# Graph attention and hyperbolic mean on one core: one folded weight matrix for the scores, normalisation moved to GpSimd

## What is computed

```python
h = relu(layernorm(x))                      # layer 0: attention inside graphs
query, key, value = h @ Wq.T + bq, h @ Wk.T + bk, h @ Wv.T + bv
a = where(mask, query @ key.T / sqrt(256), 0)
scores = (a + adj + adj) * where(mask, 1, -1e6)
x = x + (softmax(scores) * mask) @ value
h = relu(layernorm(x))                      # layer 1: weighted mean over all rows
x = x + gnn1(h, adj, W)                     # its core is adj @ (gamma * points)
```

## Time and profile before

| what | value |
|---|---|
| median of 3 runs | 795.56 us (793.64 to 797.42) |
| the profiled execution | 796.11 us |
| its span | 794.3 us |
| PE busy in the span | 740.1 us, 93% |
| DVE busy | 639.8 us, 81% |
| ACT busy | 480.7 us, 61% |
| POOL busy | 100.1 us, 13% |
| mean granted TensorE clock | 0.979 |

### The profile page before, as it was taken

How to read it: one execution, slowest core, us unless ns; L and a number is a source line. 1 busy time by engine, 2 the same in 40 slices (tenths; PEclk the granted TensorE clock), 3 DMA queues, 4 the chain that set the end, 5 groups by cost and what they waited for, 6 DMA issues and landing times.

```text
span 794.3 us, 14768 instructions
## 1 busy us (share of the span) xinstructions
PE 740.1 (93%) x4996; PEld 684.3 (86%) x4996; DVE 639.8 (81%) x1240; ACT 480.7 (61%) x879; POOL 100.1 (13%) x212
## 2 busy tenths in 40 slices
PE   4999979999999999999878899999999999999980
PEld 4888868788888888888778899999999999999980
DVE  6768577877787878889689788988888888888874
ACT  2344356787777789778654555555544555555853
POOL 0000121122111112268000000000000000000080
PEclk9999989999999999999999999999999999999995
DMA  5116268767777776679737698999899889999541
GB/s 146 54 54 239 106 246 300 273 241 253 289 289 288 281 258 253 238 255 220 171 74 154 155 204 188 202 201 199 185 218 195 189 188 190 189 192 204 120 154 63
DMA packets 53000, 157.26 MB, mean 198 GB/s; under 512 B 8656, under 2 KB 30416, under 8 KB 46800
## 3 DMA queue, kind: packets, MB, share of 16 engines
q1 hardware_dynamic: 52944, 156.60, 72.1%
HBM read 148.16 MB, written 8.42 MB: 197 GB/s over the span
## 4 chain that ended last, share of the span: by engine, by line
PE 44%; issue 28%; DVE 10%; POOLq 5%; DMA 5%; ACT 3%; DVEq 2%; POOL 1%; SPq 1%; ACTq 0%
PE bank L676 42%; DMA adjL<-in_adj 3%; DVE adjT_lo L1503 3%; DMA x_scratch<-x 1%; POOLq L600 1%; DVE bank L1495 1%; DVE turned L1495 1%; ACT adjT_hi L1018 1%; POOLq L620 1%; PE bank L668 1%; POOLq L606 1%; POOLq L550 1%; DVE X_lo L1483 1%; POOL q_low L558 1%; DMA w_raw<-in_L_gnn_Wv 1%
## 5 line engine op out<-in xcount | busy, mean ns | idle before, releaser
L676 PE MATMUL bank<-X_hi,adjT_hi 128*128 128x258 f32 x1024 | 291.6, 285 | 14.2 <-DVE adjT_lo L1503 14.2
L676 PE MATMUL bank<-X_lo,adjT_hi 128*128 128x258 f32 x1024 | 290.8, 284 | 0.0
L676 PE MATMUL bank<-X_hi,adjT_lo 128*128 128x258 f32 x1024 | 290.2, 283 | 0.0
L676 PEld LDWEIGHTS bank<-X_hi,adjT_hi 128*128 128x128 f32 x1024 | 194.4, 190 | 16.7 <-DVE adjT_lo L1503 13.6
L676 PEld LDWEIGHTS bank<-X_lo,adjT_hi 128*128 128x128 f32 x1024 | 194.8, 190 | 0.0
L676 PEld LDWEIGHTS bank<-X_hi,adjT_lo 128*128 128x128 f32 x1024 | 194.6, 190 | 0.0
L822 PE MATMUL bank<-values,probT 128*128 128x256 f32 x512 | 120.7, 380 | 1.1 <-ACT probT L1142 1.1
L1018 ACT CAST adjT_hi<-turned 128x1024 fp32r<-128x1024 f32 x64 | 67.1, 1048 | 68.0 <-PE bank L676 56.5
L822 PEld LDWEIGHTS bank<-values,probT 128*128 128x128 f32 x512 | 92.9, 189 | 14.2 <-ACT probT L1142 2.1
L1018 ACT CAST adjT_hi<-bank 128x1024 fp32r<-128x1024 f32 x64 | 64.8, 1013 | 62.3 <-PE bank L676 44.2
L1495 DVE STREAM_TRANSPOSE bank<-adjL 128x1024 f32<-128x1024 f32 x61 | 76.2, 1250 | 16.3 <-DMA adjL<-in_adj 15.9
(11 more groups left out here) (195 smaller groups left out, 1125.7 us busy)
## 6 DMA issues: line engine op xcount, KB each, us to landing
adjL<-in_adj SPq DMA_DIRECT2D x120, 512.0 KB, 8.5
adjU<-in_adj SPq DMA_DIRECT2D x32, 1024.0 KB, 7.5
adjL<-in_adj SPq DMA_DIRECT2D x16, 2048.0 KB, 7.9
x_scratch<-x SPq DMA_DIRECT2D x16, 258.0 KB, 3.4
xin<-in_x SPq DMA_DIRECT2D x8, 512.0 KB, 3.9
xt<-in_x SPq DMA_DIRECT2D x16, 256.0 KB, 7.0
adj<-in_adj SPq DMA_DIRECT2D x8, 512.0 KB, 14.0
x_all<-x_scratch SPq DMA_DIRECT2D x16, 256.0 KB, 10.7
```

What stands on the lines that cost most here:

```text
L676: last = pe.matmul(dst, a[i][a_cols], b[j][b_cols], start=(k_first and n == 0), stop=(k_last and n == 2))
```

## The change

The scores are `(h Wq' + bq)(h Wk' + bk)'`. Written out they are `h (Wq' Wk) h'`, plus a term of the column that is `bq Wk h'`, plus a term of the row `h Wq' bk + bq bk'`. The kernel after makes `Wq' Wk` once (4 matmuls from the raw weights), multiplies the group's rows by it with `bq Wk` as bias, and calls that the queries. The keys are the normalised rows themselves, which are there already: the high and low parts of the turned rows in the upper four groups, and their relu in the lower ones (`keys_lower`, on ACT). The term of the row is a 257th column of the values (a 258th is a copy of it, so that the count is even): the values' weights get two more columns, `Wq' bk`, and DVE adds the row's number in `scores_lower`, `maximum_upper` and the bias of the upper exponential.

`normalise` and `diagonal` go from DVE to POOL. Statistics and normalisation of group g+2, not g+1, are made during `project(g)`. The turning of group g+1 stands between the two halves of the queries. The three weights are not turned any more but for the values'. The check of the graph borders stands behind DVE's `project(1)`, and the sums that give `graph_col` ahead of it all. The order of the first loads is kept but for the last weight `W`, which comes behind the second group of rows. Attention is otherwise as before, and the mean is not touched.

```diff
+        wT_hi = place("wT_hi", [P, 2, KD, XW], "adjL", N * 4 + 2 * BPC * D * 4, F32R)
+        wT_lo = place("wT_lo", [P, 2, KD, XW], "small", 0, F32R)
...
+        value_banks = [a[:, :].rearrange("p (j c) -> p j c", j=2)[:, :, 0:XW] for a in (bank34, bank67)]
...
+            def normalise(g):
+
+                par = g % 2
+                pool.wait_ge(s_rstd, g + 1)
+                for j in range(BPC):
+                    last = pool.tensor_scalar(xin[:, par, j, :], xin[:, par, j, :], mv[:, par, j, 0:1],
+                                              rstd[:, par, j:j + 1], ALU.subtract, ALU.mult)
+                last.then_inc(s_norm, 1)
+
+            def diagonal(g):
+
+                pool.wait_ge(s_col, 1)
+                wait(pool, s_grow_ps, g - 1)
+                for j in range(BPC):
+                    t = g * BPC + j
+                    last = pool.tensor_scalar(diag[:, g % 2, j * P:(j + 1) * P], ident_b[:, :],
+                                              graph_col[:, t:t + 1], None, ALU.mult)
+                last.then_inc(s_diag, 1)
+
+            normalise(0)
+            normalise(1)
+            diagonal(0)
+            for g in range(NG):
+                if g < NG - 2:
+                    normalise(g + 2)
+                if g < NG - 1:
+                    diagonal(g + 1)
+            pool.wait_ge(s_kq, KD * (NG // 2 + 1))
...
+            pe.wait_ge(s_wqk, 16 * 2)
+            for k in range(KD):
                 for h in range(KD):
...
+                    last = pe.matmul(bank[2][:, k * D:(k + 1) * D], w_raw[:, 0, h, k * P:(k + 1) * P], w_raw[:, 1, h, :],
+                                     start=(h == 0), stop=(h == KD - 1))
+            last.then_inc(s_fold_ps, 1)
+            pe.wait_ge(s_wv, 16)
+            for h in range(KD):
+                for k in range(KD):
+                    last = pe.transpose(bank[3][:, k * D + h * P:k * D + (h + 1) * P],
+                                        w_raw[:, 2, h, k * P:(k + 1) * P], ident[:, :])
+            last.then_inc(s_wt_ps, 1)
+
+            def folded_biases():
+
+                pe.wait_ge(s_wide, 1)
+                for k in range(KD):
+                    for h in range(KD):
+                        pe.matmul(bank[4][:, k:k + 1], w_raw[:, 1, h, k * P:(k + 1) * P], bqk[:, 0, h:h + 1],
+                                  start=(h == 0), stop=(h == KD - 1))
+                for k in range(KD):
+                    for h in range(KD):
+                        pe.matmul(bank[4][:, KD + k:KD + k + 1], w_raw[:, 0, h, k * P:(k + 1) * P], bqk[:, 1, h:h + 1],
+                                  start=(h == 0), stop=(h == KD - 1))
+                for h, wide in enumerate((near_part, far_part)):
+                    last = pe.matmul(bank[4][:, 2 * KD:2 * KD + 1], wide[:, :], bqk[:, 1, h:h + 1], start=(h == 0),
+                                     stop=(h == KD - 1))
+                last.then_inc(s_rest_ps, 1)
+
...
+                wait(pe, s_kl, KD * min(g, NG // 2))
...
             def project(g, par):
+
+                gu = g - NG // 2
+                if gu < 0:
+                    parts, h_cols = (hT_hi, hT_lo), lambda k, a, b: (every, par, k, slice(a, b))
+                else:
+                    parts, h_cols = keysU_parts, lambda k, a, b: (every, k, slice(gu * CH + a, gu * CH + b))
                 pe.wait_ge(s_hT, KD * (g + 1))
...
+                for h in range(KD):
+                    wait(pe, s_kq, KD * (g - 1) + h + 1)
+                    if h == 0:
+                        pe.wait_ge(s_wt, 1)
+                        wait(pe, s_grow, g)
+                    for k in range(KD):
+                        last = three(bank[(2, 5)[h]][:, :], wT_parts, parts, (every, 0, k, slice(h * P, (h + 1) * P)),
+                                     h_cols(k, 0, CH), k == 0, k == KD - 1)
+                    last.then_inc(s_kq_ps, 1)
+                    if h == 0 and g < NG - 1:
+                        turn_h(g + 1, 1 - par)
+                pe.wait_ge(s_wt, 3)
                 for b in range(2):
                     if b == 1:
                         graph_numbers(g)
                     wait(pe, s_v, 2 * g + b - 1)
                     for j in range(2):
                         for k in range(KD):
-                            last = three(bank[6 + b][:, j * D:(j + 1) * D], hT_parts, wT_parts,
...
+                            last = three(value_banks[b][:, j, :], parts, wT_parts,
+                                         h_cols(k, (2 * b + j) * P, (2 * b + j + 1) * P),
+                                         (every, 1, k, every), k == 0, k == KD - 1)
                     last.then_inc(s_v_ps, 1)
...
+            folded_biases()
...
+                    to = hT_hi[:, par, k, :] if gu < 0 else keysU_hi[:, k, gu * CH:(gu + 1) * CH]
+                    act.activation(to, bank[k][:, :], ACT.Relu).then_inc(s_hT_hi, 1)
+
+            def keys_lower(g):
+                for k in range(KD):
+                    act.wait_ge(s_hT, KD * g + k + 1)
+                    act.activation(keysL[:, g * BPC:(g + 1) * BPC, k * P:(k + 1) * P],
+                                   bank[k][:, :].rearrange("p (j c) -> p j c", j=BPC), ACT.Relu).then_inc(s_kl, 1)
+
+            def queries(g, h):
+                act.wait_ge(s_kq_ps, KD * g + h + 1)
+                act.activation(qx_v[:, g, :, h * P:(h + 1) * P], bank[(2, 5)[h]][:, :].rearrange("p (j c) -> p j c", j=BPC),
+                               ACT.Identity, bias=bias_q[:, h:h + 1], scale=HALF_SCALE).then_inc(s_kq, 1)
...
-                if 0 < g < NG - 1:
-                    deviation(g + 1)
-                keys_queries(g)
+                queries(g, 0)
                 if g < NG - 1:
                     relu_h(g + 1, 1 - par)
+                if g < NG - 2:
+                    deviation(g + 2)
+                queries(g, 1)
+                if g + 1 < NG // 2:
+                    keys_lower(g + 1)
                 act.wait_ge(s_grow_ps, g + 1)
                 act.copy(graph_row[:, g * CH:(g + 1) * CH], bank[2][:, :]).then_inc(s_grow, 1)
 
             deviation(0)
...
+                wait(dve, s_norm, g - 1)
...
+            def inverse(g):
...
+                dve.reciprocal(rstd[:, g % 2], rstd[:, g % 2]).then_inc(s_rstd, 1)
...
+                    if gu < 0:
+                        to, hi = hT_lo[:, par, k, :], hT_hi[:, par, k, :]
+                    else:
+                        to, hi = keysU_lo[:, k, gu * CH:(gu + 1) * CH], keysU_hi[:, k, gu * CH:(gu + 1) * CH]
...
+            statistics(0)
+            inverse(0)
+            dve.tensor_reduce(graph_col[:, :], counts[:, :, :], AX.X, ALU.add).then_inc(s_col, 1)
+            dve.wait_ge(s_bias, 16 * 2)
+            for h, wide in enumerate((near_part, far_part)):
+                last = dve.tensor_scalar(wide[:, :], ones_b[:, :], bqk[:, 0, h:h + 1], None, ALU.mult)
+            last.then_inc(s_wide, 1)
+            weights_low(0)
+            statistics(1)
+            low_h(0, 0)
+            inverse(1)
+            dve.wait_ge(s_rest_ps, 1)
+            dve.tensor_scalar(bias_q[:, :], bank[4][:, 0:KD], HALF_SCALE, None, ALU.mult).then_inc(s_const, 1)
+            dve.tensor_scalar(row_w[:, :, :], bank[4][:, KD:2 * KD].unsqueeze(2).to_broadcast([P, KD, 2]), HALF_SCALE, None,
+                              ALU.mult)
+            dve.tensor_scalar(bv_row[:, D:XW], bank[4][:, 2 * KD:2 * KD + 1].to_broadcast([P, 2]), HALF_SCALE, None, ALU.mult)
+            weights_low(1)
...
+                if g < NG - 2:
+                    statistics(g + 2)
                 if g < NG - 1:
                     low_h(g + 1, 1 - par)
+                if g < NG - 2:
+                    inverse(g + 2)
                 for b in range(2):
                     dve.wait_ge(s_v_ps, 2 * g + b + 1)
-                    dve.tensor_tensor(val_v[:, g, 2 * b:2 * b + 2, 0:D], bank[6 + b][:, :].rearrange("p (j d) -> p j d", j=2),
-                                      bv_row[:, :, :], ALU.add).then_inc(s_v, 1)
+                    dve.tensor_tensor(val_v[:, g, 2 * b:2 * b + 2, 0:D + 1], value_banks[b][:, :, 0:D + 1],
+                                      bv_row[:, 0:D + 1].unsqueeze(1).to_broadcast([P, 2, D + 1]), ALU.add).then_inc(s_v, 1)
+                if g == 1:
+                    graph_borders()
...
+                    dve.scalar_tensor_tensor(out=near_part[:, :], in0=bank[1 + (s.par * (HC + 1) + HC) % 2][:, 0:P],
+                                             scalar=row_part(s.tile(HALFWAY)), in1=same[:, s.par, :], op0=ALU.add,
+                                             op1=ALU.mult).then_inc(s_qk_used, 1)
...
+                    if row is not None:
+                        dve.tensor_scalar(up_bias[:, par:par + 1], top[:, :], row, -2.0, ALU.subtract, ALU.mult)
...
+                    row = row_part(s.tile(HALFWAY) + HT)
+                    dve.drain()
+                    dve.tensor_scalar(top[:, :], top[:, :], row, None, ALU.add)
```

(58 more changed lines are left out.)

161 lines of the change are left out of this document (58 added, 103 removed).

## The result

The kernel after takes 790.74 us in the median of seven runs (788.19 to 792.64), the kernel before 795.56 in seven runs beside them: a ratio of 0.9936, with a 95% interval of 0.9917 to 0.9956. It is faster by 0.6%, where 2.4% were forecast, and the time lies above the range. The profiled execution took 790.15 us, its span is 788.2.

A forecast was written before the change was run, and what follows sets the result against it. PE alone was taken to bound the projection, 9.43 us per group. Terms -21.7 + 0 - 0.5 + 1.5 + 1.5 = -19.2 us gave 776.3 us against the median; 8-in-10 range 771.7 to 784 us.

The forecast's parts named there:

- The slack: Projection, row buffer's round: POOL ends normalising at 6.6 us, PE wants the rows at 8.1; 1.5 us spare, no cost.
- rival A: Projection: each POOL normalising pass waits for a DVE instruction, up to 0.69 us, delaying PE's turning; 784 us, chance 0.14.
- check of the borders: Projection: moved behind group 1, it delays group 4's statistics and PE's group 3; +1.5 us once, between 0 and 2.6.
- The start: Before the first projection group: transposes saved and small matmuls added balance; 0 us, between -0.5 and +2.5.
- Matmuls removed: Projection: 12 matmuls instead of 24 per group, less two extra value columns; 21.7 us go, a group lasts 6.7.
- 0.5 for the diagonal: First projection group: PE's wait for the diagonal goes because POOL makes it beside that group; -0.5 us, between -0.5 and 0.
- Attention: DVE's added work per step, 0.4 to 0.5 us, is paid in about four steps; +1.5 us, bounds 0.4 and 6.4.
- Rival B: Attention: DVE's addition is on the path in all 16 steps, 6.4 us instead of 1.5; 781 us, chance 0.10.
- C: Projection: row buffer's load, statistics, POOL and turning become the group, slower than before; 807 us, chance 0.03.
- D: First attention step waits for rows of adj, so the gain is only moved; 790 to 797 us, chance 0.03.
- its own upper end: Whole kernel: top of the forecast's own range, given as 781 us with the start and border check at their worst.

The follow-up runs named there:

- experiment 7: Kernel after with POOL's normalising passes in other operator orders or single operators and the diagonal from float32 (normalisation wrong); 782.34 us, single execution.
- experiment 5: Kernel after, but DVE negates the four means and POOL's normalising adds instead of subtracts; 780.34 us, ratio 0.9814 to the kernel before.
- experiment 6: experiment 5 with the check of the graph borders cut in two and moved into DVE's idle time at the start; 779.25 us, ratio 0.9806.
- experiment 9: experiment 6 with the row's number left out of attention, so the scores lack that term; 775.32 us, ratio 0.9742 to the kernel before.
- experiment 4: Kernel after with the row's number left out of attention, so the scores lack that term; 789.37 us, ratio 0.9918 to the kernel before.
- experiment 8: Kernel after with normalising back on DVE and the check of the borders moved into the start; 778.68 us, ratio 0.9802 to the kernel before.
- experiments 1: Kernel after with normalising back on DVE behind the reciprocal, the diagonal staying on POOL; 778.51 us, ratio 0.9797 to the kernel before.

## Why the prediction was wrong

**The step that failed** is "POOL gets four normalising passes; its nearest row is a pass of 128x256 with a scalar per row, 0.48 us, so 1.92 per group". It measured 4.83, and with that the step built on it failed too: "The slack is 1.5 us per group, so I count nothing." Shape, type and engine of that row were the same, its operators were not: the row behind the 0.48 adds and multiplies, the change subtracts and multiplies. The forecast took this one row and gave the pass no upper bound. A dearer row stood in the same group: the mask's pass of half the size takes 0.62, and twice that is 1.24. The forecast saw this row, bounded the diagonal with it and let it feed rival A, but did not scale it to the normalising pass. That 1.24 comes so near the 1.22 measured would have been luck: the mask's pass has one operator, and by experiment 7 a single operator takes 0.61 us on 128x128 but 0.93, not 1.22, on 128x256.

**The bookkeeping around it held.** It gave POOL 1.5 us of slack per group. The four passes took 4.83 - 1.92 = 2.91 us more, so 1.4 beyond the slack, a group of 6.7 + 1.4 = 8.1; the chain shows 8.13. Over six groups that is 8.5 us, and the projection missed its forecast by 8.2. So close a match is in part luck: the ring from 17.36 to 26.35 us, partly at half clock, lasted 0.9 more than the others and the one with the check of the borders 0.6 more, while the forecast had taken 1.5 for that check.

**Rival A** had the right symptom, PE's turning waits for POOL in every group, but the wrong cause. It let DVE hold POOL for up to 0.69 us per pass. All 32 passes of the kernel after lie between 1.214 and 1.282 us, and all 32 of experiment 5 between 0.547 and 0.682. Where the check of the borders ran beside the first group, one pass did stretch: a normalising pass to 1.338 us in experiment 6 and 1.343 in experiment 9, against medians of 0.557 and 0.553. So it seems that a pass can be held beside DVE, but in these two kernels that came once in 32 passes, and in the kernel after the pass beside the check took 1.272 us against a median of 1.220. The rule of the Trainium skill cited with it (SBUF — State Buffer, section "Who interferes with whom") confines such holding to DVE instructions with two SBUF inputs or in a two-port mode; these rows agree with it.

Another page, which the prediction did not weigh, bears on the price itself: the Trainium skill (GPSIMD Engine Reference, section "4.1 Engine selection") says of elementwise work on GpSimd that "1-input is roughly line-rate". Here the same normalisation took 0.41 us on DVE and 1.22 on POOL, 0.56 with add. The measurement decides: the rate depends on the operators.

**The start**, 0 forecast and +4.2 measured, is in the main the same error seen a second time. Normalising takes 4.92 us instead of 1.92, so PE sits idle 2.09 us ahead of 13.53; from 15.0 to 24.0 its granted clock is 0.50, 1.2 of 2.4 GHz, and the ten bias matmuls take 19.14 - 15.01 = 4.1 us, of which the relu and the low part, done at 17.17, cover only the first half. In experiment 5, with POOL in time and the clock at 1.00, the projection starts at 15.70, and in experiment 6, where the bias matmuls take 2.3, at 15.67: +0.7, within the forecast's -0.5 to +2.5. What is left there goes back to a reading of the order that held in the kernel after but not once POOL was in time, that DVE's second statistics end while ACT is still at the relu: in experiment 5 ACT is done with it at 13.79, DVE's aggregates start at 14.09 and the low part follows at 14.47, and PE waits 0.9 us for it.

**Matmuls removed** were right. Experiment 6, which has neither POOL's delay nor the borders' round in its projection, takes 77.11 - 54.34 = 22.8 us less there than the kernel before; the forecast's 21.7 and 0.5 for the diagonal make 22.2. The clock moves this by more than a microsecond: the kernel before ran 3.2 us of its projection at half clock and experiment 6 none, and experiment 9, with the same projection and a slower start, takes 77.11 - 56.12 = 21.0 less.

**The check of the borders** went where the forecast said: in experiment 5 it stands in the chain, and PE's group 3 waits 0.8 us for the graph row. Its cost, 55.41 - 54.34 = 1.1 us, is under the 1.5 taken. In the kernel after it lengthened one ring, to 8.69 us (34.48 to 43.17) from 8.13.

**Attention** was taken a little low: 2.7 us by experiment 4 and 1.5 at least by experiment 9, against 1.5. PE waited for DVE's chunk six times, 6.7 us in all, instead of three times and 4.4 before; three to five steps were forecast. Where the work is paid it costs more than the 0.4 us taken: in the first step the stretch from DVE's first to its fifth chunk takes 14.19 us after (85.48 to 99.67) and 13.40 before (93.82 to 107.22). **Rival B** fell: ten steps, from the start of the lower minimum in step 2 to that in step 12, take 174.55 us after and 173.31 before, 0.12 per step where B wanted 0.4. **C** stayed out: the ring is 8.13 us, under the 9.43 of before. As in C, slow passes on POOL made a round the group, but it was another round: C's goes through the row buffer's load and needed passes of 3 us, this one goes through turning, relu, low part and reciprocal and closed at 1.22. **D** fell: no first chunk waited for a load. One sum of the prediction does not come out: its own upper end, the start at +2.5 and the check at 2.6 together, is 779.9 us, or 780.4 with the diagonal's 0.5 not gained, not 781.

**Not settled:** the mean's stage, where nothing was changed, took 413.85 to 417.03 us in these profiles. That noise of some 3 us was counted nowhere. The profiled execution of experiment 5, 780.51 us, misses the forecast of 776.9 by 3.6: 2.3 in the mean, 1.6 in attention and 0.7 at the start, less 1.0 in the projection. What moves the mean was not tried, nor why POOL is slower with subtract.

## What to carry to other kernels

When work moves to another engine, the price is that of its operators on that engine, not of its shape: look for a row with the same pair of operators, and if there is none, take both the quickest and the slowest row of that engine, scaled to the size as a rough bound, and follow the slow one through the order. Two rows of one engine that contradict each other by size are a warning that something else sets the price.

Look for rings: when a product's consumer stands ahead of the next round's producer on the same engine, that producer's delay comes back in every round. Here POOL had 6.7 - 3.3 = 3.4 us per group: what lay beyond that was paid in every group, and less than that cost nothing.

A helping engine in a chain can be repaired with algebra: negating four means on DVE made 32 passes 2.2 times as fast.

## What the runs showed of the hardware

On POOL a tensor-scalar pass of 128x256 in float32 takes 0.48 us for add with a constant and mult by a row's scalar, 0.55 to 0.56 for add and mult by two row scalars in either order, 0.93 for mult or subtract alone, and 1.16 to 1.23 for the pairs of subtract and mult. Adding a zero behind a lone multiplication made the diagonal quicker, 0.375 us against 0.606. A single multiplication or comparison of 128x128 takes 0.60 to 0.62. A tensor-tensor subtraction on POOL is not slow: L589 of the kernel after takes 0.684 us and the addition of L621 0.806, at the same shape, though L589 writes float32r and L621 float32.

The granted clock at the start differed between executions, and PE's idle time ahead of the first group does not explain it alone. After waits of 2.09 us in the kernel after and 1.61 in experiment 8 it was 0.50 (15.0 to 24.0 us) and 0.66 (15 to 25 us). But after 0.81 us in experiment 9 it was 0.50 (15 to 20 us), and after 0.69 in experiment 6 and 0.90 in experiments 1 and 5 it was 1.00 (15 to 25 us). What decides was not tried. The clock row is not always sure either: for 15 to 25 us of experiment 4 it reads 1.00, while the first matmuls of its projection start 0.43 us apart, as in the kernel after, where it reads 0.50. What half the clock costs the ten bias matmuls is plain: 4.1 us against 2.3.
